# A two-layer graph transformer on one core: edge loops written out, a one-hot comparison against PSUM, weights loaded during the edge stage

## The reference

```python
h = maximum(layernorm(x), 0)
for l in range(2):
    k, q, v = (typed_linear(h, ntype, W[l]) for W in (Wk, Wq, Wv))   # 8 types, 128 x 128 each
    a = (rel_apply(k[src], etype, Watt[l]) * q[dst]).sum(-1) * pri[l][:, etype].T / sqrt(16)
    alpha = softmax of a over the edges of one destination
    agg = segment_sum(alpha * rel_apply(v[src], etype, Wmsg[l]), dst)
    out = silu(typed_linear(agg, ntype, Wa[l]))
    al = sigmoid(skip[l][ntype])
    out = out * al + h * (1 - al)
    h = layernorm(out) * ln_g[l] + ln_b[l]
result = x + h @ Wff + bff
```

## Time and profile before

| | |
|---|---|
| time before, median of 3 runs | 3047.16 us |
| profiled execution: its own time, its span | 3049.51 us, 3047.8 us |
| busy in the span: PE, DVE, ACT, POOL | 2005.9 (66%), 2014.2 (66%), 1791.0 (59%), 2039.5 us (67%) |
| lists and node_stage 0 | 0 to 410 us |
| edge_stage 0, and node_stage 1 | 410 to 1465, and to 1768 us |
| edge_stage 1, and node_stage 2 | 1768 to 2823, and to 3047 us |
| the 1568 edge gathers on POOL | 1556.7 us busy, 476.7 us idle ahead of them |
| granted PE clock, whole span | 0.754 of full |

### The profile page before, as it was taken

The page is one execution under the profiler, slowest core; times in us unless marked ns, Lnnn a source line. Parts: engine busy times, 40 slices in busy tenths (PEclk is TensorE's granted clock), DMA queues, the critical chain, the costliest instruction groups (busy, mean ns, idle before and its releaser), DMA issues. The chain is left out here.

```text
span 3047.8 us, 63640 instructions
## 1 busy us (share of the span) xinstructions
PE 2005.9 (66%) x12612; PEld 1716.2 (56%) x12612; DVE 2014.2 (66%) x5057; ACT 1791.0 (59%) x6727; POOL 2039.5 (67%) x2064
## 2 busy tenths in 40 slices
PE   1847747666667667666477746776766776676366
PEld 1734536666666656665355546666656666665244
DVE  7976546676766767666366656666666676765376
ACT  0026536666766666666466626666666666667254
POOL 3615467777777777775166677777777777774266
PEclk8569777777877787787587778777788777777555
DMA  4728666655656555564466666655556655663511
GB/s 115 116 92 326 281 212 182 179 177 175 180 178 181 174 173 178 179 178 124 133 261 248 262 182 179 180 181 173 177 178 178 181 174 173 179 178 89 163 40 33
DMA packets 427377, 529.02 MB, mean 174 GB/s; under 512 B 71241, under 2 KB 342155, under 8 KB 414612
## 3 DMA queue, kind: packets, MB, share of 16 engines
q0 software_dynamic: 102144, 327.28, 33.7%
q1 hardware_dynamic: 293720, 183.50, 20.8%
q10 hardware_dynamic: 31248, 15.75, 2.0%
HBM read 393.41 MB, written 150.71 MB: 179 GB/s over the span
## 5 line engine op out<-in xcount | busy, mean ns | idle before, releaser
L1267 POOL DMA_INDIRECT g_rows<-node_kv,g_ids x1568 | 1556.7, 993 | 476.7 <-issue 461.0
L1517 PE MATMUL g_ps_q<-g_qw,g_hot_t 128*128 128x128 f32 x3136 | 623.5, 369 | 85.3 <-DMA g_qw<-node_q 41.9
L1301 DVE TENSOR_TENSOR g_rows<-g_rows,g_ps_q 128x512 f32<-128x512 f32 x448 | 275.0, 614 | 588.5 <-DMA g_rows<-node_kv,g_ids 569.8
L1517 PEld LDWEIGHTS g_ps_q<-g_qw,g_hot_t 128*128 128x128 f32 x3136 | 562.0, 272 | 107.0 <-DVE g_rows L1301 49.2
L1437 ACT ACTIVATE acc<-acc,g_gained,g_scale x1568 | 606.2, 387 | 5.3 <-issue 3.5
L1498 PE MATMUL g_ps_sum<-g_hot,g_rows 128*128 128x128 f32 x3136 | 537.2, 324 | 33.4 <-ACT acc L1437 33.3
L1498 PEld LDWEIGHTS g_ps_sum<-g_hot,g_rows 128*128 128x128 f32 x3136 | 498.3, 239 | 48.9 <-ACT acc L1437 47.0
L1428 ACT ACTIVATE g_gained<-g_ps_sum,g_scale 128x1 f32<-128x1 f32 x1568 | 385.4, 246 | 75.8 <-issue 72.1
L1432 ACT ACTIVATE acc<-g_ps_sum 128x127 f32 x1568 | 415.6, 265 | 1.8
L1506 PE MATMUL g_ps_hot<-ident,g_hot_t 128*128 128x128 f32 x1568 | 280.5, 301 | 54.7 <-ACT g_hot L1442 54.2
L1455 ACT ACTIVATE g_exp_t<-g_shifted 112x128 f32<-112x128 f32 x112 | 34.7, 310 | 432.4 <-DVE g_shifted L1320 432.4
(11 more groups left out here) (249 smaller groups left out, 3277.2 us busy)
## 6 DMA issues: line engine op xcount, KB each, us to landing
g_qw<-node_q SPq DMA_DIRECT2D x1568, 64.0 KB
g_rank_row<-edge_rank SPq DMA_DIRECT2D x114, 448.0 KB, 4.6
g_rows<-node_kv,g_ids POOLq DMA_INDIRECT x1568
node_h<-n_norm SPq DMA_DIRECT2D x112, 64.0 KB
n_h<-node_h ACTq DMA_DIRECT2D x14, 512.0 KB, 7.3
node_agg<-n_agg SPq DMA_DIRECT2D x24, 256.0 KB, 3.5
node_rows<-node_x SPq DMA_DIRECT2D x2, 1792.0 KB
node_q<-l_blank_q SPq DMA_DIRECT2D x1, 3200.0 KB
```

What stands on the lines that cost most here:

```text
L1267: g_.indirect_dma_start(out=rows[j][:, g, :], out_offset=None, in_=scratch["kv"][:, :], in_offset=bass.IndirectOffsetOnAxis(ap=ids[half][: ...
L1301: v.tensor_tensor(half, half, ps_q[k % 2][:, 0:len(four), :], ALU.mult).then_inc(s["prod"], 1)
L1517: ins = t.matmul(ps_q[k % 2][:, n, :], hot_t[j % 2][:, g, :], qw[j % 2][:, g, :], start=True, stop=True)
```

## The change

1. **Loops.** `over` in the edge stage, and POOL's loop, become Python loops: every batch is written out, all waits compare with constants. POOL's `sem_inc(s["go"])` after its waits goes.
2. **PSUM operands.** The one-hot comparison becomes a `tensor_tensor` of the ranks (SBUF) with the number column, which is copied to PSUM once and broadcast. `fwd`, `upto` and the reciprocal move from SBUF to PSUM (bank `ps_a`). Since that bank is PE's output bank too, PE now waits for `alpha` before the matmul that writes `ends_ps`.
3. **Loads.** The linears live in constants' tensors; layer 0's are loaded by ACT while the lists are made, the next stage's by SP at the start of each edge stage, as the first DMAs after the ranks. `skip`, `ln_g`, `ln_b` as columns are loaded once, with the lists. In a node stage `h`, the other small tensors and `xr` are issued by SP, between and after the stores of the groups.
4. **Roots.** One more step of lead: the node pipeline starts at step -9, everything up to the variances moves one step earlier, ACT's root is one step after DVE's variances and one before DVE's inverses.
5. `tab["type"]` is bf16; the gates get a tensor of their own.

```diff
@@ edge_stage
-        fwd, top, shifted, exp_t, upto, total, alpha = (sb(n, [GH, P]) for n in (...))
+        top, shifted, exp_t, total, alpha = (sb(n, [GH, P]) for n in ("top", "shifted", "exp_t", "total", "alpha"))
+        fwd, upto, number_ps = ps_a[0:GH, 2 * P:3 * P], ps_a[0:GH, 3 * P:4 * P], ps_a[:, 2 * P - 1:2 * P]
+        inverse = fwd
-        def over(engine, body, after, count=B):
-            for j in range(U):
-                body(0, j, j)
-            with engine.Fori(1, count // U) as i:
-                for j in range(U):
-                    body(i, j, i * U + j)
+        def over(body, after, count=B):
+            for b in range(count):
+                body(b // U, b % U, b)
...
                 ranks(0, 0)
+                load_linears(sp, c, weights, l + 1)
...
                             pool.wait_ge(s["sums"], (b - U) * NF + g // FOUR + 1)
-                            pool.sem_inc(s["go"], 1)
...
-                    v.tensor_scalar(hot_t[u][:, :, :].rearrange("p g e -> p (g e)"), rank_row[u][:, :], c["number"][:, 0:1], None,
+                    v.tensor_tensor(hot_t[u][:, :, :].rearrange("p g e -> p (g e)"), rank_row[u][:, :], number_ps.to_broadcast([P, G * P]),
                                     ALU.is_equal).then_inc(s["hot_t"], 1)
...
                         pe.wait_ge(s["ends"], 2 * mid[0] + 2)
+                        pe.wait_ge(s["alpha"], mid[0] + 1)
                         t.matmul(ends_ps, ...)
-                        pe.wait_ge(s["alpha"], mid[0] + 1)
@@ load_linears (new)
+    if l < L:
+        for n, name in enumerate(("Wk", "Wv", "Wq")):
+            engine.dma_start(c["w_all"][:, :, n, :], weights[name][l].rearrange("t i o -> i t o")).then_inc(c["w_in"], 16)
+    if l > 0:
+        engine.dma_start(c["wa_all"][:, :, :], weights["Wa"][l - 1].rearrange("t i o -> i t o")).then_inc(c["w_in"], 16)
@@ node_stage, SP
                         load(a_d[:, k * ABOUT:k * ABOUT + n, :], agg[k % 4][:, 0:n, :], a_out[k % 4])
+                        if k == 0:
+                            load(h[:, 0:TL, :], tiles(scratch["h"], 0), rows_in[0])
+                    for n in range(1, LOADS):
+                        load(h[:, n * TL:(n + 1) * TL, :], tiles(scratch["h"], n), rows_in[n])
+                if last:
+                    load(gain_in...), load(shift_in...), load(bff...), load(wff...)      # s["w_small"], four
+                    load(xr[:, :, :], scratch["rows"].rearrange("(t p) d -> p t d", p=P), s["xr"])
@@ node_stage, DVE (the other engines alike)
-                    if real(i + 6):
-                        moments(i + 6)
-                        if (i + 6) % 4 == 3:
-                            variances((i + 6) // 4)
+                    if real(i + 7):
+                        moments(i + 7)
+                        if (i + 7) % 4 == 3:
+                            variances((i + 7) // 4)
@@ node_stage, ACT
-                    if real(i + 2) and (i + 2) % 4 == 0:
-                        root((i + 2) // 4)
+                    if real(i + 3) and (i + 3) % 4 == 0:
+                        root((i + 3) // 4)
```

More of the change, by code:

```diff
@@ L710, in over @@
         def over(step):
-            for i in range(-8, TT):
+            for i in range(-9, TT):
                 step(i)
@@ L1135, in step @@
                 def step(i):
-                    if real(i + 7 + AG) and not first:
-                        gather(i + 7 + AG)
+                    if real(i + 8 + AG) and not first:
+                        gather(i + 8 + AG)
                     if real(i + 1) and not last:
@@ L1274, in _ @@
                 number(0, 0)
-                eight(0, 0)
-                with pool.Fori(1, B // AHEAD) as i:
+                for i in range(B // AHEAD):
                     eight(i * AHEAD, i * 2)
@@ L1409, in end @@
                         step(B // U - 1, n, B - U + n)
-                over(dve, step, end, B - U)
+                over(step, end, B - U)
             @block.scalar
@@ L1482, in end @@
                         step(B // U, n, B + n)
-                over(act, step, end)
+                over(step, end)
                 act.wait_ge(s["joined"], T)
@@ L1558, in end @@
                         step(B // U, n, B + n)
-                over(pe, step, end)
+                over(step, end)
 CHAIN = 16
```

121 lines of the change are left out of this document (55 added, 66 removed).

## The result

| | before | after |
|---|---|---|
| median of the runs, us | 3057.0 (4 runs, 3036.9 to 3069.0) | 2920.9 (4 runs, 2916.3 to 2921.4) |
| profiled execution, us | 3049.5 | 2921.0 |
| first to last gather, edge stage 0 and 1, us | 1018.2 and 1018.4 | 984.0 and 981.2 |
| granted clock of it, mean | 0.754 | 0.775 |

The ratio is 0.954, 95% interval 0.950 to 0.958: 4.6% faster; the kernel before was run once more beside the changed one, which moves its median from 3047 to 3057. The profiled executions differ by 128.6 us; the prediction had 124.6, and 2925 us.

A forecast was written before the change was run, and what follows sets the result against it. POOL's gathers were taken to bound the edge stages; start chains, POOL's DMA issues and root stalls the node stages. 68.6 + 13 + 15 + 24 + 4 = 124.6 off 3049.5 gave 2925 us, range 2893 to 2972.

The forecast's parts named there:

- Part 1: Edge stages: a comparison reading PSUM no longer holds POOL's gathers, 0.66 us per comparison; 68.6 us off.
- The prediction's stand-in: Edge stage: the scaling of messages, 2.00 us with a PSUM operand and no hold on gathers, taken for the new comparison.
- The rival of the scan: Edge stages: the hold moves to scan L1327, gathers wait its whole 0.41 us; 46 instead of 4.8, total 2966; 10%.
- the scan's term: Edge stages: a quarter of the L1327 scans hold a gather for 0.17 us; 4.8 us kept, bounds 0 and 19.
- Parts 2 to 4: Edge stages: written-out loops, PE's wait for alpha ahead of `ends_ps` and linears loaded on SP; each costed at nothing.
- Part 5: Start of node_stage 1: gather 17 us earlier with ACT free of loads, less 1.3 and 2.5; net 13 off.
- Part 6: Start of node_stage 2: DVE's wait for the four small tensors shortens; 15 us off, bounds 5 and 22.
- Part 7: Roots a step ahead: 24 us off, 17 in node_stage 2 and 7 in node_stage 1; bounds 8 and 40.
- Part 8: Node_stage 0: Wq loaded earlier and an earlier root; 4 us off, bounds 0 and 7.

The follow-up runs named there:

- two_sbuf: The changed kernel with the comparison still a `tensor_tensor`, but its number operand from SBUF; 3073.5 us, 1.1% over the kernel before.
- undo_unroll: The changed kernel with the edge stage's loops as hardware loops again on all five queues; 2924.0 us, ratio to before 0.959.
- only_compare: The kernel before with the one-hot comparison alone changed to a `tensor_tensor` against a PSUM column; 2986.4 us, ratio 0.980.
- undo_loads: The changed kernel with every weight loaded by ACT at the start of its node stage again; second chip, 3576.8 us, ratio to before 0.951.
- compare_and_scans: The kernel before with the PSUM comparison, the scans' PSUM operands and PE's earlier wait for alpha; second chip, 3838.0 us, ratio 1.022.
- undo_compare: The changed kernel with the comparison alone put back to a `tensor_scalar` against the SBUF column; 2993.6 us, ratio to before 0.984.
- undo_compare_again: The changed kernel with the comparison as a `tensor_scalar` from SBUF, on a fourth chip; 3479.1 us, ratio to before 0.943.

## Why the prediction was right

| part | predicted | measured in the two traces |
|---|---|---|
| 1 to 4, both edge stages | -68.6 | -71.4 |
| 5, start of node_stage 1 | -13 | -12.1 (-16.9 lead in, +4.8 fill) |
| 6, start of node_stage 2 | -15 | -11.1 (-25.1 lead in, +14.0 fill) |
| 7, node_stage 2 steady | -17 | -18.6 |
| 7, node_stage 1 steady | -7 | -16.6 |
| 8, up to the first gather of edge stage 0 | -4 | +1.5 |
| sum | -124.6 | -128.3 |

**Part 1** is shown by two runs in both directions: alone it gives 34 and 36 us off the edge stages, taken away it gives 33 and 33 back. The price per comparison, 0.66 us from the earlier trace rows, was a little high: of the 73.4 us in that trace 68.8 stand at the 112 comparisons, 0.61 each, and 4.2 in 28 gathers that begin inside a scan, mostly L1329, as the one of the earlier trace rows. The change took these away too, so the sum did not suffer. What I did not see is the mechanism in full. The prediction's stand-in was the scaling of messages, which has a PSUM operand too, and it gave the right answer. It left open what decides, and `two_sbuf` tells: the same instruction of 2.02 us holds gathers for 142 us with its operand in SBUF and for 2 with it in PSUM. The Trainium skill, "SBUF — State Buffer", section "Who interferes with whom", states that an instruction with two SBUF inputs contends with a GpSimd instruction that reads SBUF, as its second input comes through the shared read interface, and that one with at most one SBUF input outside the 2-port modes does not. The trace agrees with both. The same section infers that a `tensor_tensor` would not stall a DMA's descriptor generation; the 142 us of `two_sbuf` speak against that for these gathers. The trace also shows the order: a gather is held if the comparison began ahead of it, and not if it had begun 0.02 us or more ahead of the comparison. What holds gathers in the `tensor_scalar`, its fast form or the SBUF column that it reads beside the ranks, no run here separates.

**The rival of the scan** rested on two ends, 0.17 and 0.41 us; the few gathers over 1.05 us (10 of 1568, the longest 1.14) are the near end, and rarer than assumed: 1.7 us in long gathers, against 4.8. All ten begin inside L1327, as this one:
```profile
1081.04 0.43 DVE L1327 TENSOR_TENSOR_SCAN g_ps_a<-g_same,g_exp_t 112x128 f32<-112x128 bf16 x1
1081.07 1.14 POOL L1268 DMA_INDIRECT g_rows<-node_kv,g_ids  x1 [0.30 <-issue]
```
That the scan's term came out near 2 and not 4.8 makes the difference between 68.6 and 71.4. The scan does hold a gather to its own end, as the rival had it, but costs less than its 0.42 us: the gather ends 0.75 us behind the scan (1082.21 and 1081.47 here; 0.75 too in the earlier trace rows), and a free one 0.95 behind its own start. So a gather that starts x into a scan of 0.42 loses 0.22 - x, an estimate from these rows, and beyond 0.22 nothing; for the gather of the earlier trace rows that is 0.17, as measured. Against the comparison of `two_sbuf`, which a held gather outlasts by 0.82, the same sum gives 2.02 + 0.82 - 0.95 - x = 1.89 - x, so at most 2.84 us for a gather, and the longest took 2.85.

**Parts 2 to 4** at nothing, on this chip: `undo_unroll` shows it for the loops, and `only_compare`, which lacks the scans' PSUM operands and PE's earlier wait and has the same edge stages within 1 us, for these. The loads on SP delayed PE's first spread: it waits 25.51 us, before 19.34, 6.2 more, and the edge stage did not see it. The prediction had 5 to 7, covered.

**Part 5** came out term by term: lead in 17 (16.9). Fill was charged 1.3 + 2.5 and took 4.8: the fifth to seventh gathers wait 1.04 to 1.44 us for PE, and SP was issuing the pieces of `h` until 1456.3. That the pieces of `h` are the reason is likely and not shown. `undo_loads` found the lead in again on another chip, 15 to 17 us.

**Part 6** has nearly the right sum (15 against 11.1) from wrong terms, which is luck. DVE's first linear comes 17.0 us behind its gates and 31 us behind the stage's first store, not 27 to 28. I placed the small tensors behind 13 stores and 7 pieces of `h` at 0.9 and 1.77 us; the stores took 11.8 in all, as I took them, but SP's issue of `gain_in` alone took 2.17 us, and the last of the four landed some 6 us behind its issue at 2750.32. From the edge stage's last gather DVE's first linear comes at 68.6 us, before at 77.8: 9 earlier and not 14. The first gather came 25 earlier, and the fill takes 14 of these back.

**Part 7** in node_stage 2 is shown by the intervals (4.25 to 2.85 once in four tiles, 13 times 1.4 is 18), though no run of the first chip undid the roots alone. In node_stage 1 the term was undersized: 16.6 and not 7. A late root made some 7 on the third chip. The other 9 stay open: the window's granted clock is 0.87 now and was 0.80, and the intervals of three tiles in four, not of one, were well over 4 us (medians 4.74, 3.96, 4.45, 4.88; after, 3.95 to 4.18). On the first chip every kernel with loads and roots moved has 225 to 230 and every one without 244 to 248, but none with one of the two.

**Part 8** failed in its sign, within its size: the first q scatter came 3.6 us earlier as predicted, but first to last took 201.8 instead of 196.4. That stretch ran between 195.6 and 223.7 us in six traces of the first chip with no pattern by edit, so 4 us cannot be read there.

What the prediction lacked is its condition. It named DVE's slack of over 4 us a batch as the cover of the longer comparison, and POOL as the bound because it waited 0.3 us at most. On a chip where POOL waits for PE, the comparison made no gain that shows (`compare_and_scans`, 1.022), and by elimination the loops that I costed at nothing carry most of the gain that is left. So the number holds for a chip like that of the trace; on the others the change as a whole wasn't timed, and its variants there gained 4 to 6%, by other terms.

## What to carry to other kernels

Where GpSimd's indirect DMAs set the pace, look for the DVE instructions that a long one overlaps, and ask where their inputs lie before asking how long they take: one operand in PSUM made a comparison 0.85 us slower and the kernel 2% faster, while the same instruction with both inputs in SBUF made it 1.1% slower than before. Ahead of a chain that a load releases, put the small tensors first in the issuing queue, but expect what was behind them to ask for its share. And a term costed at nothing, because its engine waits anyway, holds for the chip whose waits were read: the written-out loops were worth 0 on one chip and, by elimination, some 110 us a stage on another.

## What the runs showed of the hardware

- A `tensor_scalar` of bf16 against an SBUF column (1.15 us) holds a gather that is under way until 0.12 us behind its end, if that gather began up to 0.52 us ahead of it, and one that begins inside until 0.81 to 0.83 behind. One that began 0.53 us or more ahead is free, and it is the comparison that takes longer then, 1.33 us at most and less the earlier the gather began (`before`, `undo_compare`).
- A `tensor_tensor` with two SBUF inputs (2.02 us) holds gathers that begin inside it, until 0.82 us behind its end; those begun 0.02 us or more ahead are free (`two_sbuf`). With one input in PSUM it holds none (`after`; the few long gathers there are held by the scan that follows).
- A scan of 0.42 us with both inputs in SBUF holds a gather that begins inside it until 0.75 us behind the scan's end; only those that begin in its first 0.2 us lose by it, 0.2 us at most (`before`, `after`).
- The same kernel took 3048 us on one chip and 3679 to 3756 on three others, and its variants took 3479 to 3838 there. Their gathers, comparisons and joins last as long as on the first chip; the granted clock of the edge stages is lower (0.69 to 0.76 against 0.79 to 0.83), and ACT and PE stand still with no releaser named. The hold by the comparison is there as well (`undo_compare_again`, 95 long gathers). Whether the lower clock is a cause or comes of the stalls is open, and so is the cause of these.
